# A graph network's relational pass: which turn of the group loop each quad's message sums stand in

## What is computed

```python
x = _layernorm(x + _L0_gnn_ref(x, edge_index, ...))                 # five attention convolutions
x = _layernorm(x + _L1_gnn_ref(x, edge_index, edge_type_4, W, attn)) # the relational pass
x = _layernorm(x + _L2_gnn_ref(...))                                # two plain convolutions
x = _layernorm(x + _L3_gnn_ref(...))                                # weighted edges
```

```python
alpha = jnp.sum(cat * a, axis=-1)
alpha = jnp.where(alpha > 0, alpha, NEG_SLOPE * alpha)
seg = edge_types * N + dst
m = jax.ops.segment_max(alpha, seg, num_segments=S)
alpha_exp = jnp.exp(alpha - m[seg])
denom = jax.ops.segment_sum(alpha_exp, seg, num_segments=S)
w = alpha_exp / denom[seg]
msg = (src_feat * w[..., None]).reshape(E, H * D)
out = jax.ops.segment_sum(msg, dst, num_segments=N)
```

## Time and profile before

| | |
|---|---|
| three runs | 5794.07 us median, 5793.05 to 5795.5 |
| the profiled execution | 5796.47 us |
| its span (first to last instruction) | 5794.7 us |
| mean granted clock of PE | 0.687 of 2.4 GHz |
| busy share of the span: PE, PEld | 63%, 50% |
| DVE | 58% |
| ACT | 26% |
| POOL | 70% |
| the relational pass's edge stage | about 3315 to 4103 us |

### The profile page before, as it was taken

The page is one execution under the profiler, slowest core; times in us unless marked ns, Lnnn a source line. Parts: engine busy times, 40 slices in busy tenths (PEclk is TensorE's granted clock), DMA queues, the critical chain, the costliest instruction groups (busy, mean ns, idle before and its releaser), DMA issues. The chain is left out here.

```text
span 5794.7 us, 84655 instructions
## 1 busy us (share of the span) xinstructions
PE 3630.9 (63%) x17936; PEld 2901.8 (50%) x17937; DVE 3388.3 (58%) x9194; ACT 1522.0 (26%) x3590; POOL 4078.2 (70%) x4168
## 2 busy tenths in 40 slices
PE   5667756666677667666888746666644444446555
PEld 3556545553666356554566536656533333334334
DVE  7777756664666556655666466666443344336665
ACT  4334323432334224332454422222100010000000
POOL 4477577776777677777777667666577767766775
PEclk6877768877767777777898855555655555558778
DMA  7556265645556266535665433331122122211111
GB/s 238 172 173 182 87 205 171 189 126 150 176 173 179 78 197 184 171 104 176 175 180 164 106 73 69 66 70 42 40 53 53 53 62 52 53 48 57 52 53 52
DMA packets 631578, 681.11 MB, mean 118 GB/s; under 512 B 178675, under 2 KB 512969, under 8 KB 631145
## 3 DMA queue, kind: packets, MB, share of 16 engines
q0 software_dynamic: 166480, 384.64, 23.8%
q1 hardware_dynamic: 464792, 293.21, 17.4%
HBM read 620.51 MB, written 56.89 MB: 117 GB/s over the span
## 5 line engine op out<-in xcount | busy, mean ns | idle before, releaser
L618 POOL DMA_INDIRECT kvconv<-kv_tab,src_all x1664 | 1627.9, 978 | 645.0 <-issue 499.6
L618 POOL DMA_INDIRECT rowsg_<-h_tab,src_all x832 | 788.8, 948 | 322.5 <-issue 252.9
L632 POOL DMA_INDIRECT lst_tab<-pay,ord_now x416 | 432.8, 1040 | 215.1 <-issue 124.9
L618 POOL DMA_INDIRECT rows_r<-rel_tab,idx_r x416 | 419.4, 1008 | 202.8 <-issue 113.4
L618 POOL DMA_INDIRECT rowss_<-h_tab,dst_i_g x416 | 397.9, 957 | 161.0 <-issue 119.5
L618 POOL DMA_INDIRECT kvlast<-kv_tab,src_all x416 | 409.7, 985 | 133.4 <-issue 123.1
L1061 ACT ACTIVATE Sconv<-s8conv 128x512 f32<-128x512 fp8e4 x384 | 240.8, 627 | 396.1 <-PE pA1conv L1019 285.0
L1123 DVE TENSOR_TENSOR msgconv<-kvconv,sm_attEconv 128x512 f32<-128x512 f32 x416 | 286.1, 688 | 80.2 <-PE pA0conv L1019 27.7
L1019 PEld LDWEIGHTS pA0conv<-Sconv,msgconv 128*128 128x128 f32 x1664 | 300.7, 254 | 13.1
L1019 PEld LDWEIGHTS pA1conv<-Sconv,msgconv 128*128 128x128 f32 x1664 | 291.4, 247 | 17.0
L1019 PE MATMUL pA0conv<-Sconv,msgconv 128*128 128x128 f32 x1664 | 299.7, 340 | 0.0
(11 more groups left out here) (655 smaller groups left out, 8960.0 us busy)
## 6 DMA issues: line engine op xcount, KB each, us to landing
qwinconv<-q_tab SPq DMA_DIRECT2D x1664, 64.0 KB
kvconv<-kv_tab,src_all POOLq DMA_INDIRECT x1664
st8conv<-st_tab SPq DMA_DIRECT2D x52, 512.0 KB
s8conv<-s_tab SPq DMA_DIRECT2D x52, 512.0 KB
qwinlast<-q_tab SPq DMA_DIRECT2D x416, 64.0 KB
kv_tab<-stageconv_n SPq DMA_DIRECT2D x28, 512.0 KB
rowsg_<-h_tab,src_all POOLq DMA_INDIRECT x832
q_tab<-stageconv_n SPq DMA_DIRECT2D x28, 256.0 KB
```

The lines of the kernel that those rows point to most:

```text
L618: nc.gpsimd.indirect_dma_start(rows[:, par * TG + t, :], None, tab, bass.IndirectOffsetOnAxis(ap=idx[:, g * TG + t:g * TG + t + 1], axis=0 ...
L632: nc.gpsimd.indirect_dma_start(lst_tab, bass.IndirectOffsetOnAxis(ap=ord_now[:, i:i + 1], axis=0), pay[:, i, :], None).then_inc(sem("liste ...
```

## The change

The two constants of distance become tables from the turn to the quads that are handled in it. For the sums, with the distances counted back from the turn:

| turn | 0 | 1 | 2 | 3 | 4 | 5 | 6 | 7 |
|---|---|---|---|---|---|---|---|---|
| sums before | quad 3 | 4 | 5 | 6 | 7 | 0 | 1 | 2 |
| sums after | quad 2 | 3 | 4, 5 | 6, 7 | 0 | 1 | none | none |
| evictions before | quad 2 | 3 | 4 | 5 | 6 | 7 | 0 | 1 |
| evictions after | quad 2 | 3 | 4, 5 | 6, 7 | none | 0 | 1 | none |

In turns 0 to 3 these are quads of the group two back; in turns 4 to 7 quad 0 and those after it belong to the group one back. In turns 2 and 3 PE's sums now stand ahead of `turns_between`. ACT's evictions now stand after `scatter_cast`, still ahead of the copy of the weights. DVE's `read_added` and `rescale` move one turn earlier.

```diff
-            SUM = LAG + 1
+            SUMS = {4: [12], 5: [12], 0: [14], 1: [14], 2: [14, 13], 3: [13, 12]}
+            OUTS = {5: [13], 6: [13], 0: [14], 1: [14], 2: [14, 13], 3: [13, 12]}
             OUT = LAG + 2
...
                     def turn(g, q, par):
-                        after, late = (shifted(g, q, par, by) for by in (3, -SUM))
+                        after = shifted(g, q, par, 3)
+
+                        def due():
+                            for by in SUMS.get(q, []):
+                                late = shifted(g, q, par, -by)
+                                if late:
+                                    sums(*late)
                         if started(g):
                             turns_first(pe, sm, tag, q, par, g - 1, pM)
                         if after:
                             scores(*after)
+                        if q in (2, 3):
+                            due()
                         if started(g):
                             turns_between(pe, sm, tag, q, g - 1, pM, pM)
-                        if late:
-                            sums(*late)
+                        if q not in (2, 3):
+                            due()
...
-                        far, late, last = (shifted(g, q, par, by) for by in (4, -LAG, -OUT))
+                        far, late = (shifted(g, q, par, by) for by in (4, -LAG))
...
                         if late:
                             sum_cast(*late)
-                        if last:
-                            put_out(*last)
                         if far:
                             scatter_cast(*far)
+                        for by in OUTS.get(q, []):
+                            last = shifted(g, q, par, -by)
+                            if last:
+                                put_out(*last)
...
-                        reads = q in (5, 6) and not (isinstance(g, int) and (g < 2 or g > GROUPS))
+                        reads = q in (4, 5) and not (isinstance(g, int) and (g < 2 or g > GROUPS))
...
-                        if q == 5 and reads:
+                        if q == 4 and reads:
...
-                        if q == 6 and reads:
+                        if q == 5 and reads:
                             rescale(g - 1)
```

## The result

| | before | after |
|---|---|---|
| median (lowest to highest), 4 runs each on one chip | 5794.56 us (5793.05 to 5795.5) | 5733.17 us (5731.32 to 5736.52) |
| ratio, 95% interval | | 0.9894 (0.9881 to 0.9907) |
| the profiled execution, its span | 5796.47, 5794.7 us | 5731.77, 5729.9 us |
| mean granted clock of PE | 0.687 | 0.684 |
| first gather of the pass to the next stage's first load | 3315.43 to 4103.67: 788.2 us | 3311.61 to 4036.92: 725.3 us |

The change saves 61.4 us of medians, 64.8 us of the two spans. The stage gives 62.9 of the latter; it begins 3.8 us earlier in this profile, and what follows it is 2.0 us longer (1693.0 against 1691.0).

What follows compares the result with a forecast made beforehand. Bound: a chain of DVE's softmax and PE's backlog, 54.4 us a group, POOL behind it at 48.4. Removing 55.4 us of POOL waits ends the stage at 4035.9, not 4103.42: 67.5 saved, 5729.0 profiled, 5727 median; range 5717 to 5760.

Steps and rivals of the forecast that it cites:

- Turns 2 and 3: Pairs of quads fill PE's holes before L495 (7.79 us) and L521 (7.65 us); L502 starts 1.3 us earlier.
- Turns 4 to 7: Between L521 and L478 PE has two quads instead of five: 10.6 us instead of 19.65, about 8.4 us saved.
- The chain alone: DVE's softmax and PE's backlog, waiting on each other: period falls from 54.4 to about 46 us a group.
- POOL as the bound: POOL's 32 gathers and 5 list writes a group, 48.4 us, become the limit; 55.4 us of its waits go.
- The step that failed: Stage's end: last list write at 4034.5 plus 1.4 us to land, so the stage ends at 4035.9, 67.5 us saved.
- PE's end: End of PE's work in the stage, with the last eviction: 4021.6, 14 us before POOL.
- A: Rival: pairs don't quite fit turns 2 and 3, each microsecond of misfit lengthening the period; 5751 us, chance 0.22.
- B: Rival: denser DVE work slows POOL's issues; if the excess of 0.07 us an issue doubles, 5758 us, chance 0.07.
- C: Rival, slower: pairs before L495 and L521 start only after DVE's scans, period 60.6 us; 5857 us, chance 0.04.
- D: Rival, no change: another wait, say window loads behind the later S load, holds the period near 54; 5783 to 5794, chance 0.03.

Runs made afterwards that it cites:

- best version: Changed kernel with four list writes a group instead of five, ten in the start-up, 36 after the last gather, ten in each of two later blocks: 5698.13 us.
- start-up version: Changed kernel with seven of the 53 last list writes moved into GpSimd's start-up wait: 5722.82 us, ratio 0.9876 to the kernel before.

## Why the prediction was right, and by how much it was off

It said 5727, the runs 5733.17. The signs, the mechanism and the new bound were those forecast; how close the total came is partly luck, since two errors at the stage's end and in GpSimd's issues (9.1 and 4.6 us, below) stand against each other, and the profiled stage also began 3.8 us earlier than in the kernel before, which nothing in the prediction covers (what follows it was 2.0 longer).

- **Turns 2 and 3.** Forecast: 0.5 and 0.35 us of idleness left before L495 and L521. Measured: 0.47 and 0.95 in the period shown, 0.39 to 0.67 and 0.48 to 0.95 in all groups behind the first. From L478 to L521 it is 34.3 us, against 35.0 - 1.3 = 33.7.
- **Turns 4 to 7.** Forecast: PE needs 10.6 us from the weights to the next L478. In the period shown L478 came 13.8 us behind L521, and PE had been idle for the last 3.6 of them, waiting for the logits: so it needed 10.2.
- **The chain alone.** Forecast about 46 with the loop's boundary; 45.2 in the early groups, 45.6 on average where the lists don't stand in GpSimd's way.
- **POOL as the bound.** Forecast 48.4 a group and no waits but the start-up's; measured 48.0 to 49.0 and 16.5 us of waits, 13.7 of them at the start-up. Between the first gather and the last list write the stage lost 60.0 us (774.5 to 714.5). The forecast was 55.4; the rest is about the issues' own time, 1.001 and 0.997 us instead of 1.008 and 1.014: 416 x 0.007 + 118 x 0.017 = 4.9.
- **The step that failed.** "With 1.4 us to land, as in the wait at 4016.66, POOL is through at 4035.9." The landing was right: the drain starts 1.3 us behind the last write. But POOL was not through: its drain takes 9.28 us more, and the next stage starts 10.8 us behind the write. The prediction thereby gave the change 13.5 - 1.4 = 12.1 us at the end, where it got 13.8 - 10.8 = 3.0. That is 9.1 us too much, 4.6 too little stand against it, and 67.5 becomes 63.0, where 62.9 were measured. The drain was there to be read in the trace of the kernel before: 9.28 us at L1500, and 3.48 of the 7.6 us of idleness before the pass's first gather are the drain of the block before. I looked for what waited at the end, and a drain hidden by a busier engine is not waited for.
- **PE's end.** Forecast 4021.6; the last eviction ended at 4014.2 in a stage that began 3.8 us earlier, so 3.6 us sooner than forecast, and without effect.

The rivals: **A** (the pairs don't fit) fell; PE's misfit is under 1 us a group, and the period went down when GpSimd was relieved. **B** fell too: DVE's busy time in the 50 us window rose from 32.8 to 40.0 us, and POOL's mean issue fell to 1.001. The Trainium skill (SBUF — State Buffer, section "SBUF: two separate sides") limits its rule to DVE operations in a two-port mode and, for those with two SBUF inputs, to a GpSimd operation that reads SBUF. Which of this pass's DVE operations fall under it no run here shows, so the fall of B neither confirms nor refutes the rule; the traces do show that in the kernel after an issue beside a 128x512 TENSOR_TENSOR took 1.05 us on average, one beside no DVE instruction 0.96. **C** needs the pairs behind the scans: shown by hand at 56.5 us a period where 60.6 was forecast, absent in the change. **D** did not happen; no window load held a score for long.

## What to carry to other kernels

Where two engines pass a chain to and fro, put backlog work ahead of the instruction that waits, in pieces as long as the hole: here the same pairs were 96 us faster ahead of that instruction than behind it, at equal work. Then ask which in-order queue stands right behind the shortened chain and what it carries that could run elsewhere, since that queue takes the rest of the gain. And when an engine becomes the last of its stage, count its end with the drain of its queue, read at the line of the block, not with its last instruction.

## What the runs showed of the hardware

**GpSimd's drain is long and not constant.** It took 9.28 us at the block's end in the kernels before and after, with the pairs behind, with one quad ahead, and with DVE's pieces late. It took 9.04 us with 46 list writes behind the last small loads, 8.71 with 36, and 4.38 where all 118 stood behind the last gather. PE's took 4.03 us, DVE's 0.73, ScalarE's 0.65. In blocks in which GpSimd issues nothing but list writes it was 0.86 us after 10 of them (best version), 2.82 after 34 and 3.48 after 42, some 0.083 us each; the 4.38 us are 53 times that, the list writes behind the last small loads. In the other versions 4.9 to 5.7 us come on top, and what sets those wasn't found.

**A chip on which the same kernel takes a third longer.** The start-up version ran in 5722.82 us on one chip and in 7537.47 on another. GpSimd's and DVE's instructions took no longer on the second (in the pass, the mean gather 1.000 and 0.974 us, DVE's weighing 0.685 us on both); the waits between them did. SyncE's queue was slower: a run of twenty window loads was issued over 14.4 us in a middle group on the first and over 32.9 us on the second. Between its loads stand register instructions, of 0.03 to 0.05 us on the first; on the second many took 0.7 us. From the first to the last L480, 137 of 845 of them took over 0.5 us there, and none on the first. Why, and how much of the third comes from it, wasn't tested.
